# Two attention layers, one core: the masked mean taken from a copy's running sum, and layer 0's value matmuls in pairs of key groups

## The chip, the cores and the metric

The kernel runs on one core of one Trainium2 chip. The metric is device microseconds of one execution, median of several runs. TensorE (PE in the profile) does the matmuls, ScalarE (ACT) exponentials and copies, VectorE (DVE) maxima, reciprocals and sums, GpSimd (POOL) sums and powers, SyncE (SP) issues DMAs.

## The reference, cut to what matters

```
# layer 0, 8 heads of 32, x: (16, 256, 512), mask: (16, 512)
q = xt @ Wq.T                       # one projection serves as query, key and value
logits = (scores * cmask + (1 - cmask) * NEG) * rmask   # rmask: row of the query
attn = softmax(logits);  ctx = attn @ qh;  out = ctx @ Wo.T;  x = x + out
# layer 1, 16 heads of 32: rms norm, modulation, qkv, softmax(q k), o + o @ W_out;  x = x + ...
```

A row whose own mask is 0 has all logits 0, so its softmax is even over all 512 keys and its context is the plain mean of q over time. A row whose mask is 1 attends only to keys whose mask is 1. The kernel needs both: values of masked-in keys, and the mean over all of them.

## The kernel before, in words

The 16 batches go through a software pipeline of 19 iterations (-1 to 17). A steady iteration `i` (1 to 14) works on three batches at once: layer 0 attention of batch i (segments A, heads 0 to 3, and B, heads 4 to 7), layer 1 of batch i-1 (projections `qk` and `values1`, segment C), the output projection `out1` of batch i-2, and the first projection and first maxima of batch i+1. Iterations -1, 0, 15, 16 and 17 are written out on their own.

Each engine has its own queue, and its order is written out by hand, in `iteration` and its special cases. Semaphores join them. `Order` tables (BIG for the bank PX, MAXES for the four banks PM, VISITS, CONTEXT_TAKEN) turn the order into the counts to wait for; moving a call means moving its entry there.

Layer 0 of a batch: `load_x` (SP) brings x into XB and the mask into CBM. `sums_x` (L1559, VectorE) sums each row of x over time into XS. `mask_x` (L1935 GpSimd, in iteration -1 L1554 VectorE) multiplies XB by the mask. `project0` (L398, TensorE) multiplies by Wq into PX, twice (mt = 0, 1). `take_query` (ScalarE) copies PX to QF. `project_mean` (L406) multiplies the sums XS by the same weights: four matmuls of one column, eight records in the profile, since a float32 matmul shows as two. `mean0` (L1078) scales them to MEAN. `round_query` rounds QF to QHI, `split0` (L1590, VectorE) takes QLO = QF - QHI, and SP stacks both into A0 and B0 (`stack0`). `maxima0` (L422 TensorE, L1565 VectorE) bounds each row's score. `score0` (L453) makes one head's 128 keys by 512 queries, `exp0` (L1048) takes the exponential into E. `values0` (L414) transposes QF into V0.

`values_weighted0` (L480) is one visit to TensorE's tiling of 32 columns: four heads, each 128 keys by 32 columns, side by side, over one group of 128 keys; four groups in a segment add up in bank PO. `weights_summed0` (L491) and layer 1's `values_and_sums1` (L502, L505) use the same tiling. `maxima0` and `maxima1` (L431) use the tiling of 32 rows. All else uses the whole array. `add_keys0` (L1583 VectorE, L1948 GpSimd) adds the groups' E for the softmax sums. `take_sums0`, `invert0` (L1603), `scale0` (L1608, L1954) and `context0` (L1614) write the context into XB, with MEAN where the mask is 0; `out0` (L519), `residual0` (L1621), `squares` (L1157), `mean_square` (L1627), `rstd`, `norm` (L1161, L1631), `norm_rows` (L530) and `modulate` lead into layer 1.

E has three buffers for groups of keys; `buffer_free` makes `exp0` and `exp1` wait until the group held before has been visited and added.

Of the kernel before, what the change touches and what calls it, by code (L numbers as in the profile page):

```python
# [9 lines left out]
ALU = mybir.AluOpType  # L10
# [29 lines left out]
class Order:  # L40
# [29 lines left out]
    def place(self, key):  # L70
# [66 lines left out]
    (("q1", 3), 0, QUAD), (("n0", 1), 0, 0), (("tq", 0), -1, 1), (("tq", 1), -1, 2), (("s0", 0), 0, 3),  # L137
# [7 lines left out]
            (("q1", 3), 0, QUAD), (("n0", 1), 0, 0), (("tq", 0), -1, 1), (("tq", 1), -1, 2), (("s0", 0), 0, 3),  # L145
# [13 lines left out]
            (("q1", 0), 0, QUAD), (("q1", 1), 0, QUAD), (("t0", 0), 0, 0), (("q1", 2), 0, QUAD), (("t0", 1), 0, 3),  # L159
            (("q1", 3), 0, QUAD), (("n0", 1), 0, 0), (("tq", 0), -1, 1), (("tq", 1), -1, 2), (("s0", 0), 0, 3),  # L160
# [40 lines left out]
def cond_resid(nc, x, cond, cond_t, wq_t, wo_t, w_emb, b_emb_t, g_norm_t, w_qkv, g_q_t, g_k_t, w_out, out):  # L201
# [6 lines left out]
    with ctx:  # L208
# [32 lines left out]
        XS = sb("XS", [P, 2])  # L241
        MEAN = sb("MEAN", [P, 2, NB])
# [52 lines left out]
        xs_done = ev("xs_done", 1)  # L295
        xm_done = ev("xm_done", 2)
        cbi_done = ev("cbi_done", 1)
        p0_full = ev("p0_full", 3)
# [67 lines left out]
        def _(pe):  # L366
# [27 lines left out]
            def project0(i, b, mt):  # L394
                pe.wait_ge(xm_done.sem, xm_done.at(b))
                big(("p0", mt), i)
                for c in range(2):
                    last = mm(PX[:, :], WQ[:, c, mt * P:(mt + 1) * P], XB[:, c, :], start=(c == 0), stop=(c == 1))  # L398
                last.then_inc(p0_full.sem, 1)

            def project_mean(i, b):
                big(("mean", 0), i)
                pe.wait_ge(xs_done.sem, xs_done.at(b))
                for mt in range(2):
                    for c in range(2):
                        last = mm(PX[:, mt:mt + 1], WQ[:, c, mt * P:(mt + 1) * P], XS[:, c:c + 1],  # L406
                                  start=(c == 0), stop=(c == 1))
                last.then_inc(p0_full.sem, 1)
# [170 lines left out]
            def iteration(i):  # L579
# [24 lines left out]
                step_a(0, 2)  # L604
                if o1:
                    values_and_sums1(i - 1, i - 2, 3)
                if l0:
                    maxima0(i, i, 1, 0)
                step_a(0, 3)
                if l1:  # L610
                    qk(i, 1, 0)

                step_a(1, 0)
                if l1:
                    qk(i, 1, 1)
                step_a(1, 1)
                if l1:
                    qk(i, 1, 2)
                step_a(1, 2)
                if l1:  # L620
                    qk(i, 1, 3)
                step_a(1, 3)
                if l0:
                    maxima0(i, i, 1, 1)
                    values_weighted0("A", i, 0, 0)

                step_a(2, 0)
                if l1:
                    qk(i, 2, 0)
                step_a(2, 1)  # L630
                if l1:
                    qk(i, 2, 1)
                step_a(2, 2)
                if l0:
                    maxima0(i, i, 1, 2)
                if l1:
                    qk(i, 2, 2, 3)
                step_a(2, 3)
                if l0:
                    values_weighted0("A", i, 0, 1)  # L640
                    maxima0(i, i, 1, 3)

                step_a(3, 0)
                if l1:
                    qk(i, 3, 0)
                step_a(3, 1)
                if l1:
                    qk(i, 3, 1, 2)
                step_a(3, 2)
                step_a(3, 3)  # L650
                if l0:
                    rows0(i, i, 1)
                if l1:
                    qk(i, 3, 3)
                if l0:
                    values_weighted0("A", i, 0, 2)
                if p0:
                    project0(i, i + 1, 0)

                step_b(0, 0)  # L660
                step_b(0, 1)
                if l1:
                    heads_rows(i, i - 1, 0)
                    heads_rows(i, i - 1, 1)
                if p0:
                    project0(i, i + 1, 1)
                step_b(0, 2)
                if l0:
                    weights_summed0("A", i, 0)
                step_b(0, 3)  # L670

                step_b(1, 0)
                if l1:
                    heads_rows(i, i - 1, 2)
                    heads_rows(i, i - 1, 3)
                step_b(1, 1)
                step_b(1, 2)
                if l0:
                    values_weighted0("A", i, 0, 3)
                if p0:  # L680
                    project_mean(i, i + 1)
                if l1:
                    maxima1(i, i - 1, 0)
                step_b(1, 3)
                if l0:
                    values_weighted0("B", i, 1, 0)

                step_b(2, 0)
                step_b(2, 1)
                if o1:  # L690
                    out1(i, i - 2, 0, 0)
                if l1:
                    maxima1(i, i - 1, 1)
                if o1:
                    out1(i, i - 2, 0, 1, 2, 3)
                step_b(2, 2)
                if l1:
                    maxima1(i, i - 1, 2)
                if l0:
                    values_weighted0("B", i, 1, 1)  # L700
                if o1:
                    out1(i, i - 2, 1, 0, 1)
                step_b(2, 3)
                if l1:
                    maxima1(i, i - 1, 3)

                step_b(3, 0)
                if o1:
                    out1(i, i - 2, 1, 2, 3)
                step_b(3, 1)  # L710
                step_b(3, 2)
                if l1:
                    rows1(i, i - 1)
                if l0:
                    values_weighted0("B", i, 1, 2)
                if p0:
                    maxima0(i, i + 1, 0, 0)
                step_b(3, 3)
                if l1:
                    values1(i, 0, 0, 1, 2)  # L720
# [8 lines left out]
                step_c(0, 2)  # L729
                if l1:  # L730
                    values1(i, 1, 0)
                step_c(0, 3)
                if l1:
                    values1(i, 1, 1)
                if p0:
                    maxima0(i, i + 1, 0, 1)
# [3 lines left out]
                if l1:  # L740
                    values1(i, 1, 2)
                step_c(1, 2)
                if l1:
                    values1(i, 1, 3)
                step_c(1, 3)

                step_c(2, 0)
                if p0:
                    maxima0(i, i + 1, 0, 2)
                if l1:  # L750
                    values_and_sums1(i, i - 1, 0)
                if l0:
                    out0(i, i, 0)
                    out0(i, i, 1)
                step_c(2, 1)
                step_c(2, 2)
                step_c(2, 3)
                if p0:
                    maxima0(i, i + 1, 0, 3)
                if l1:  # L760
                    values_and_sums1(i, i - 1, 1)

                step_c(3, 0)
                step_c(3, 1)
                if p0:
                    rows0(i, i + 1, 0)
                step_c(3, 2)
                step_c(3, 3)
                if l0:
                    norm_rows(i, i)  # L770
                if l1:
                    values_and_sums1(i, i - 1, 2)

            def iteration_before(i):
                project0(i, i + 1, 0)
                maxima0(i, i + 1, 0, 0)
                project0(i, i + 1, 1)
# [5 lines left out]
                maxima0(i, i + 1, 0, 3)  # L783
                modulation(3)
                project_mean(i, i + 1)
                rows0(i, i + 1, 0)
                modulation(4)
                modulation(5)
                modulation(6)
                modulation(7)  # L790

            def iteration_0(i):
                values0(i, i, 0)
                score0("A", i, i, 0, 0, 0)
                score0("A", i, i, 0, 0, 1)
                maxima0(i, i, 1, 0)
                score0("A", i, i, 0, 0, 2)
                score0("A", i, i, 0, 0, 3)
                score0("A", i, i, 0, 1, 0)
                score0("A", i, i, 0, 1, 1)  # L800
                maxima0(i, i, 1, 1)
                score0("A", i, i, 0, 1, 2)
                score0("A", i, i, 0, 1, 3)
                project0(i, i + 1, 0)
                score0("A", i, i, 0, 2, 0)
                maxima0(i, i, 1, 2)
                score0("A", i, i, 0, 2, 1)
                values_weighted0("A", i, 0, 0)
                score0("A", i, i, 0, 2, 2)
                values_weighted0("A", i, 0, 1)  # L810
                maxima0(i, i, 1, 3)
# [1405 lines left out]
```

## Time and profile before

| | |
|---|---|
| median of 3 runs | 1326.3 us (1326.19 to 1329.03) |
| the profiled execution, its own time | 1324.62 us |
| its span, first to last instruction | 1322.8 us |
| mean granted TensorE clock | 0.972 of full speed |
| PE, PEld, DVE, ACT, POOL busy | 95%, 45%, 80%, 59%, 58% |
| DMA | 143.03 MB, mean 108 GB/s |

A row of the timeline names its start, its length, engine, line and operation, output and inputs, and how many instructions were merged; a matmul's end is modelled, so the distance between the starts of two rows is a better measure of what the first one takes.

### The profile page before, as it was taken

To read this page: it belongs to the slowest core of one execution; us is meant where nothing else is said; L and a number is where in the kernel's file an instruction comes from. 1 tells how busy PE (TensorE), PEld (TensorE's weight loads), DVE (VectorE), ACT (ScalarE), POOL (GpSimd) and SP (SyncE) were. 2 spreads that over 40 slices of the span, in tenths; PEclk is the share of its full clock that TensorE was granted. 3 is DMA by queue.
4 is the path that set the end of the run, shared out by engine and by line. 5 is a ranking of instruction groups with operands and counts; after the bars stand their busy time and mean duration, and the time that the engine had idled before them with its cause. 6 is when DMAs were issued, how large, how long until landed. Compare 5 with 4: busy or idle time off the path is not lost.

```text
span 1322.8 us, 20986 instructions
## 1 busy us (share of the span) xinstructions
PE 1261.4 (95%) x6896; PEld 597.6 (45%) x6896; DVE 1055.8 (80%) x934; ACT 774.6 (59%) x1377; POOL 764.4 (58%) x389
## 2 busy tenths in 40 slices
PE   6969899999999999999999999999999999999987
PEld 4424444444444454444445444444444444444433
DVE  6756778888887887888788788878888887888654
ACT  1626565665656566565656666565666656566523
POOL 0337467475746747484674748467474856638452
PEclk8859899999999999999999999999999999999999
DMA  8321534525264452626445252634525263441322
GB/s 288 105 65 47 136 105 96 140 54 151 74 148 109 99 138 56 149 72 150 107 107 131 60 147 70 153 104 112 130 60 145 69 156 100 113 110 44 97 59 70
DMA packets 77962, 143.03 MB, mean 108 GB/s; under 512 B 21536, under 2 KB 23072, under 8 KB 77856
## 3 DMA queue, kind: packets, MB, share of 16 engines
q1 hardware_dynamic: 69136, 126.17, 38.1%
q10 hardware_dynamic: 8720, 15.51, 4.0%
q8 instruction: 59, 0.97, 0.3%
q14 instruction: 47, 0.39, 0.1%
HBM read 32.02 MB, written 8.39 MB: 31 GB/s over the span
## 4 chain that ended last, share of the span: by engine, by line
PE 88%; ACT 4%; DVE 2%; issue 2%; SPq 1%; ACTq 1%; POOL 1%; DMA 0%; DVEq 0%
PE PX L541 25%; PE PS L453 11%; PE PO L480 9%; PE PX L575 8%; PE PO L502 5%; PE PS L467 4%; PE PX L398 4%; PE PM L422 4%; PE PX L519 2%; PE PM L491 2%; PE PM L519 2%; PE PM L559 2%; PE PM L431 2%; PE PO L505 2%; ACT E L1055 2%
## 5 line engine op out<-in xcount | busy, mean ns | idle before, releaser
L1048 ACT ACTIVATE E<-PS,KBIAS 128x512 f32<-128x512 f32 x512 | 345.3, 686 | 236.8 <-PE PS L453 221.9
L541 PE MATMUL PX<-WQKV,XNT 128*128 128x512 f32 x768 | 382.4, 602 | 3.4 <-ACT QK L1026 2.1
L1948 POOL TENSOR_TENSOR E<-E 128x1024 f32<-128x1024 f32 x112 | 263.4, 2359 | 160.8 <-PE PO L480 92.9
L1565 DVE TENSOR_REDUCE NM<-PM 128x4 f32<-128x2048 f32 x128 | 291.3, 2276 | 52.3 <-PE PM L422 52.3
L453 PE MATMUL PS<-B,A 97*128 97x512 f32 x512 | 301.7, 624 | 5.3 <-ACT E L1048 4.9
L1978 POOL TENSOR_TENSOR KQLO<-E 128x1024 f32<-128x1024 f32 x64 | 151.2, 2363 | 211.3 <-ACT E L1055 209.5
L1960 POOL TENSOR_TENSOR RQK<-RQK,HALF 128x16 f32<-128x16 f32 x64 | 201.0, 3148 | 28.3 <-DVE RQK L1653 27.5
L1572 DVE TENSOR_REDUCE NM<-PM 128x8 f32<-128x2048 f32 x64 | 146.6, 2291 | 49.1 <-PE PM L431 49.0
L541 PEld LDWEIGHTS PX<-WQKV,XNT 128*128 128x128 f32 x768 | 137.8, 192 | 91.4 <-issue 75.7
L1055 ACT ACTIVATE E<-PS 128x512 f32<-128x512 f32 x256 | 145.3, 596 | 49.0 <-PE PS L467 48.3
L453 PEld LDWEIGHTS PS<-B,A 97*128 97x128 f32 x512 | 95.6, 192 | 148.1 <-issue 123.6
L480 PE MATMUL PO<-E,V 128*32 128x512 f32 x1024 | 139.5, 617 | 0.0
L467 PE MATMUL PS<-B,A 97*128 97x256 f32 x512 | 124.4, 350 | 8.8 <-ACT E L1055 8.2
L1672 DVE RECIPROCAL T<-T 128x256 f32<-128x256 f32 x64 | 111.5, 1742 | 12.4 <-ACT T L1026 12.4
L575 PE MATMUL PX<-WOUT,OT 128*128 128x512 f32 x248 | 120.5, 605 | 0.0
L467 PEld LDWEIGHTS PS<-B,A 97*128 97x128 f32 x512 | 77.2, 188 | 80.2 <-issue 53.1
L1603 DVE RECIPROCAL R<-R 128x256 f32<-128x256 f32 x64 | 109.8, 1736 | 1.1
L1583 DVE TENSOR_TENSOR E<-E 128x1024 f32<-128x1024 f32 x80 | 97.7, 1238 | 11.9 <-ACT E L1048 10.1
L1935 POOL TENSOR_TENSOR XB<-XB,CBM 128x512 f32<-128x512 f32 x30 | 37.8, 1281 | 72.6 <-DVE XS L1559 56.6
L422 PE MATMUL PM<-QHI 32*128 32x512 f32 x512 | 67.1, 513 | 10.5 <-DVE NM L1565 6.9
L1646 DVE TENSOR_REDUCE SSQ<-YSQ 128x16 f32<-128x512 f32 x64 | 42.8, 669 | 40.2 <-ACT YSQ L1116 40.1
L398 PE MATMUL PX<-XB,WQ 128*128 128x512 f32 x128 | 65.6, 637 | 8.0 <-DVE XB L1554 8.0
(84 smaller groups left out, 1408.2 us busy)
## 6 DMA issues: line engine op xcount, KB each, us to landing
A<-QHI SPq DMA_DIRECT2D x256, 64.0 KB, 2.0
B<-QHI SPq DMA_DIRECT2D x256, 64.0 KB, 2.0
A<-KQHI SPq DMA_DIRECT2D x128, 128.0 KB, 2.3
B<-KQHI SPq DMA_DIRECT2D x128, 128.0 KB, 2.4
XB<-x SPq DMA_DIRECT2D x16, 512.0 KB, 3.9
A<-QLO SPq DMA_DIRECT2D x128, 64.0 KB, 2.0
B<-QLO SPq DMA_DIRECT2D x128, 64.0 KB, 2.0
X<-x ACTq DMA_DIRECT2D x16, 512.0 KB, 5.4
```

Of the source, the lines that this page charges most:

```text
L453: mm(PS[n % 2][:, :], A0[0:97, h, g * P:(g + 1) * P], B0[0:97, h, :], start=True, stop=True).then_inc(score_full, 1)
L467: last = mm(PS[n % 2][:, kb * N1:(kb + 1) * N1], A1[0:97, hq, c, kb * P:(kb + 1) * P], B1[0:97, hq, c, :], start=True, stop=True)
L480: last = mm(PO[h * DH:(h + 1) * DH, :], V0[:, q, g, h * DH:(h + 1) * DH], E[:, probs(seg, i, g), h, :], start=(g == 0), stop=(g == KB0 - 1))
L541: last = mm(PX[:, :], XNT[:, c, t * P:(t + 1) * P], WQKV[:, c, part * DM:(part + 1) * DM], start=(c == 0), stop=(c == 3))
L575: last = mm(bank, OT[:, c, t * P:(t + 1) * P], WOUT[:, c, :], start=(c == 0), stop=(c == 3))
L1048: fn(E[:, probs(seg, i, g), h, :], PS[n % 2][:, :], ACT.Exp, bias=KBIAS[:, g, b:b + 1], scale=SCALE).then_inc(exp_done, 1)
L1055: fn(E[:, probs("C", i, c), h, :], PS[n % 2][:, :], ACT.Exp, scale=SCALE_RAW).then_inc(exp_done, 1)
L1565: v.tensor_reduce(NM0[:, q, :].rearrange("p (h k) -> p h k", k=KB0)[:, :, kb], PM[:, :, :], axis=AX.X, op=ALU.max, negate=True).then_inc(m ...
L1572: v.tensor_reduce(NM1[:, :].rearrange("p (h c a) -> p h c a", c=Q1, a=2)[:, :, c, :], PM[:, :, :].rearrange("p h (a k) -> p h a k", a=2), ...
L1948: g_.tensor_tensor(running(seg, i)[:, heads_, :], running(seg, i)[:, heads_, :], E[:, probs(seg, i, g), heads_, :], ALU.add).then_inc(done, 1)
L1960: g_.tensor_tensor(rqk, rqk, HALF[:, :], ALU.pow).then_inc(rqk_done.sem, 1)
L1978: g_.tensor_tensor(key_sums(c), e[:, :, 0:N1], e[:, :, N1:2 * N1], ALU.add).then_inc(esum_done.sem, 1)
```

## The change

The mean. `project_mean`, `mean0`, `sums_x` and `mask_x` go. `project0` now multiplies x as it is; `take_query`'s copy also gives the sum of each row over time, QSUM, which is 512 times the mean of q. The mask is applied to the copy in QF, by a new `mask_query` on GpSimd, between `take_query` and `round_query`. The factor 1/512 goes into CBI.

The pairs. In iterations 1 to 14, `values_weighted0` of key groups 0 and 1 stand next to each other in TensorE's order, and so do groups 2 and 3, in both segments. Around them most of the order is written anew on all engines: on TensorE the key maxima, `qk`, `heads_rows`, `out1`, `values1`, `out0` and `values_and_sums1`; on GpSimd `scale0` ahead of segment B's sums and `rstd` behind the third `add_keys1`; on VectorE `invert0`, `invert1`, `split0` and `context1`.

```diff
-            def project_mean(i, b):
-                big(("mean", 0), i)
-                pe.wait_ge(xs_done.sem, xs_done.at(b))
...
             def project0(i, b, mt):
-                pe.wait_ge(xm_done.sem, xm_done.at(b))
+                pe.wait_ge(xin_in.sem, xin_in.at(b))
...
             def values0(i, b, mt):
-                pe.wait_ge(big_taken, BIG.upto(("p0", mt), i - 1))
+                pe.wait_ge(masked.sem, masked.at(b, mt + 1))
...
-                copy(QF[:, mt, :], PX[:, :]).then_inc(big_taken, 1)
+                fn(QF[:, mt, :], PX[:, :], ACT.Copy, accum_out=QSUM[:, mt, b:b + 1]).then_inc(big_taken, 1)
...
             def round_query(i, b, mt):
-                act.wait_ge(big_taken, BIG.upto(("p0", mt), i))
+                act.wait_ge(masked.sem, masked.at(b, mt + 1))
...
-            def mask_x(i, b):
+            def mask_query(i, b, mt):
                 pool.wait_ge(cbm_in.sem, cbm_in.at(b))
-                pool.wait_ge(xs_done.sem, xs_done.at(b))
-                for c in range(2):
-                    g_.tensor_tensor(XB[:, c, :], XB[:, c, :], CBM[:, :], ALU.mult).then_inc(xm_done.sem, 1)
+                pool.wait_ge(big_taken, BIG.upto(("p0", mt), i))
+                g_.tensor_tensor(QF[:, mt, :], QF[:, mt, :], CBM[:, :], ALU.mult).then_inc(masked.sem, 1)
```

TensorE's order in a steady iteration, the parts that the prediction speaks of:

```diff
+                step_a(2, 0)
+                if l0:
+                    values_weighted0("A", i, 0, 0)
+                    values_weighted0("A", i, 0, 1)
+                    maxima0(i, i, 1, 2)
...
+                    project0(i, i + 1, 0)
+                if l0:
+                    values_weighted0("A", i, 0, 2)
+                    values_weighted0("A", i, 0, 3)
...
+                step_b(0, 1)
+                if l0:
+                    weights_summed0("A", i, 0)
...
-                if p0:
-                    project_mean(i, i + 1)
...
+                    values_weighted0("B", i, 1, 0)
+                    values_weighted0("B", i, 1, 1)
+                if l1:
+                    maxima1(i, i - 1, 1)
...
                 if p0:
                     maxima0(i, i + 1, 0, 0)
+                if l0:
+                    values_weighted0("B", i, 1, 2)
+                    values_weighted0("B", i, 1, 3)
...
+                step_c(0, 2)
+                step_c(0, 3)
                 if l0:
                     weights_summed0("B", i, 1)
-                    values_weighted0("B", i, 1, 3)
...
+                step_c(3, 0)
+                if l0:
+                    out0(i, i, 0)
+                step_c(3, 1)
+                if l0:
+                    out0(i, i, 1)
+                if l1:
+                    values_and_sums1(i, i - 1, 1)
                 if p0:
                     maxima0(i, i + 1, 0, 3)
-                if l1:
-                    values_and_sums1(i, i - 1, 1)
-
-                step_c(3, 0)
-                step_c(3, 1)
+                step_c(3, 2)
+                if l1:
+                    values_and_sums1(i, i - 1, 2)
+                step_c(3, 3)
                 if p0:
                     rows0(i, i + 1, 0)
-                step_c(3, 2)
-                step_c(3, 3)
                 if l0:
                     norm_rows(i, i)
-                if l1:
-                    values_and_sums1(i, i - 1, 2)
```

## Rows read from the trace of the kernel before

**Rows 1.** The page's busy time: us, share of the span, instructions.

```profile
PE 1261.4 (95%) x6896; PEld 597.6 (45%) x6896; DVE 1055.8 (80%) x934; ACT 774.6 (59%) x1377; POOL 764.4 (58%) x389
```

**Rows 2.** Windows, iteration 0 and one steady: length; PE, PEld, DVE, ACT, POOL busy; clock.

```profile
36.00:99.50 63.50, 49.32 (x187) 20.09 (x187) 41.57 (x41) 27.72 (x49) 22.82 (x12) 0.69 0.31 81
...
640.42:717.39 76.97, 75.93 (x432) 35.95 (x428) 64.99 (x58) 48.29 (x86) 47.77 (x24) 1.00 0.44 111
```

**Rows 3.** Timeline of TensorE: the transposes that open iterations 2 and 14.

```profile
178.60 1.09 PE L414 MATMUL PM<-IDENT,QF 128*128 128x128 f32 x8
...
1102.32 1.09 PE L414 MATMUL PM<-IDENT,QF 128*128 128x128 f32 x8
```

**Rows 4.** Timeline of TensorE, steady iteration, around the mean's matmuls.

```profile
674.48 1.06 PE L480 MATMUL PO<-E,V 128*32 128x512 f32 x8
675.48 1.05 PE L406 MATMUL PX<-XS,WQ 128*128 128x1 f32 x8
676.46 0.50 PE L431 MATMUL PM<-KQHI 32*128 32x256 f32 x8
```

**Rows 5.** Instructions of the touched lines: ns min/median/max, first and last start.

```profile
L406 PE MATMUL PX<-XS,WQ x128: 205/250/353, 27.4 to 1138.2; 128*128 128x1 f32 x128
...
L1559 DVE TENSOR_REDUCE XS<-XB x16: 1182/1220/1221, 5.2 to 1105.3; 128x2 f32<-128x1024 f32 x16
...
L1935 POOL TENSOR_TENSOR XB<-XB,CBM x30: 1264/1282/1289, 39.3 to 1107.9; 128x512 f32<-128x512 f32 x30
...
L1157 ACT ACTIVATION_READ_ACCUMULATOR YSQ<-X x32: 184/186/202, 92.2 to 1247.9; 128x1 f32 x32
```

**Rows 6.** Timeline of ScalarE: second copy to QF and first rounding to QHI.

```profile
671.96 0.59 ACT L1026 ACTIVATE QF<-PX 128x512 f32<-128x512 f32 x1
...
688.50 0.62 ACT L1026 ACTIVATE QHI<-QF 128x512 fp32r<-128x512 f32 x1
```

**Rows 7.** Timeline of TensorE: two neighbouring column visits, then two output matmuls of iteration 17.

```profile
694.85 1.02 PE L541 MATMUL PX<-WQKV,XNT 128*128 128x512 f32 x2
695.80 1.06 PE L491 MATMUL PM<-E,ONES 128*32 128x512 f32 x8
696.69 1.04 PE L480 MATMUL PO<-E,V 128*32 128x512 f32 x8
...
1316.05 1.02 PE L575 MATMUL PX<-WOUT,OT 128*128 128x512 f32 x2
1316.91 1.02 PE L575 MATMUL PM<-WOUT,OT 128*128 128x512 f32 x2
```

**Rows 8.** The page's costliest groups: count, busy us, mean ns of one, idle before.

```profile
L1948 POOL TENSOR_TENSOR E<-E 128x1024 f32<-128x1024 f32 x112 | 263.4, 2359 | 160.8 <-PE PO L480 92.9
...
L1583 DVE TENSOR_TENSOR E<-E 128x1024 f32<-128x1024 f32 x80 | 97.7, 1238 | 11.9 <-ACT E L1048 10.1
```

**Rows 9.** Timeline: from the layer 0 output to the transposes of the norm.

```profile
705.46 1.98 PE L519 MATMUL PX<-XB,WO 128*128 128x512 f32 x4
...
710.51 0.51 PE L422 MATMUL PM<-QHI 32*128 32x512 f32 x4
710.95 1.07 PE L502 MATMUL PO<-E,V 128*32 128x256 f32 x16
...
711.07 2.29 DVE L1565 TENSOR_REDUCE NM<-PM 128x4 f32<-128x2048 f32 x1 [0.15 <-PE PM L422]
...
712.38 0.74 PE L467 MATMUL PS<-B,A 97*128 97x256 f32 x4
...
713.28 1.21 DVE L1631 TENSOR_SCALAR YSQ<-X,RSTD 128x512 f32<-128x512 f32 x1
...
714.59 1.06 PE L530 MATMUL PM<-IDENT,YSQ 128*128 128x128 f32 x8
```

**Rows 10.** Timeline, the start: ScalarE's first work and iteration 0's mean.

```profile
11.60 1.28 ACT L1026 ACT_TABLE_LOAD   x1 [11.60 <-issue]
...
66.95 1.70 PE L406 MATMUL PX<-XS,WQ 128*128 128x1 f32 x8
```

More of the change, by code:

```diff
@@ L294, in cond_resid @@
         xres_in = ev("xres_in", 16)
-        xs_done = ev("xs_done", 1)
-        xm_done = ev("xm_done", 2)
+        masked = ev("masked", 2)
         cbi_done = ev("cbi_done", 1)
-        p0_full = ev("p0_full", 3)
+        p0_full = ev("p0_full", 2)
         qhi_done = ev("qhi_done", 2)
@@ L837, in iteration_0 @@
                 score0("B", i, i, 1, 3, 0)
-                project_mean(i, i + 1)
                 score0("B", i, i, 1, 3, 1)
                 values_weighted0("B", i, 1, 1)
+                project0(i, i + 1, 1)
                 score0("B", i, i, 1, 3, 2)
@@ L868, in iteration_15 @@
+                score0("A", i, i, 0, 0, 2)
+                qk(i, 1, 0)
+                score0("A", i, i, 0, 0, 3)
+                qk(i, 1, 1)
+                score0("A", i, i, 0, 1, 0)
+                maxima0(i, i, 1, 1)
+                score0("A", i, i, 0, 1, 1)
                 qk(i, 1, 2)
+                score0("A", i, i, 0, 1, 2)
+                qk(i, 1, 3)
+                values_weighted0("A", i, 0, 0)
                 maxima0(i, i, 1, 2)
-                qk(i, 1, 3)
-                score0("A", i, i, 0, 1, 1)
@@ L899, in iteration_15 @@
                 heads_rows(i, i - 1, 0)
[L900 removed]
+                score0("B", i, i, 1, 0, 2)
+                score0("B", i, i, 1, 0, 3)
                 heads_rows(i, i - 1, 1)
[L902 to L905 removed]
+                out1(i, i - 2, 0, 2)
+                score0("B", i, i, 1, 1, 0)
                 heads_rows(i, i - 1, 2)
@@ L1251, in iteration @@
                 step_b(1, 3)
-                if p0:
-                    mean0(i, i + 1)
                 step_b(2, 0)
@@ L1320, in iteration_before @@
                 take_query(i, i + 1, 1)
+                round_query(i, i + 1, 1)
                 rows0(i, i + 1, 0)
-                mean0(i, i + 1)
-                round_query(i, i + 1, 1)
             def iteration_0(i):
@@ L1361, in iteration_0 @@
                 exp0("B", i, i, 2, 3)
+                take_query(i, i + 1, 1)
                 exp0("B", i, i, 3, 0)
-                mean0(i, i + 1)
-                round_query(i, i + 1, 1)
                 exp0("B", i, i, 3, 1)
@@ L1612, in context0 @@
                 dve.wait_ge(p0_full.sem, p0_full.at(b + 1))
-                dve.wait_ge(big_taken, BIG.upto(("mean", 0), i - 1))
-                v.scalar_tensor_tensor(out=XB[:, q, :], in0=CBI[:, :], scalar=MEAN[:, q, b:b + 1], in1=TT,
+                dve.wait_ge(big_taken, BIG.upto(("p0", q), i - 1))
+                v.scalar_tensor_tensor(out=XB[:, q, :], in0=CBI[:, :], scalar=QSUM[:, q, b:b + 1], in1=TT,
                                        op0=ALU.mult, op1=ALU.add).then_inc(ctx_done.sem, 1)
@@ L1728, in iteration @@
                 if l1:
+                    split1(i, i - 1, 1)
                     split1(i, i - 1, 2)
                     split1(i, i - 1, 3)
-                if o1:
-                    context1(i - 1, i - 2, 3)
+                if l0:
+                    invert0(i, i, 0, 1)
                 if l1:
                     maxima1(i, i - 1, 0)
-                    maxima1(i, i - 1, 1)
                 if o1:
@@ L1738, in iteration @@
                 if l1:
+                    maxima1(i, i - 1, 1)
                     maxima1(i, i - 1, 2)
-                    maxima1(i, i - 1, 3)
                 if o1:
                     residual1(i, i - 2, 1)
-                if l0:
-                    invert0(i, i, 0, 1)
+                if l1:
+                    maxima1(i, i - 1, 3)
                 if p0:
@@ L1754, in iteration @@
                     invert0(i, i, 1, 0)
-                    invert0(i, i, 1, 1)
                 if p0:
@@ L1758, in iteration @@
                 if l0:
+                    invert0(i, i, 1, 1)
                     scale0(i, i, 1)
@@ L2003, in iteration @@
                     power_heads(i, i - 1, 3)
+                if l0:
+                    masked_out(i, i)
+                if l1:
                     norm_heads(i, i - 1, 3)
+                if p0:
+                    mask_query(i, i + 1, 0)
+                    mask_query(i, i + 1, 1)
                 if l0:
+                    scale0(i, i, 0)
                     add_keys0("B", i, 1, False)
                     add_keys0("B", i, 1, True)
+                    add_keys0("B", i, 2, False)
                     add_keys0("B", i, 2, True)
-                    add_keys0("B", i, 2, False)
                     add_keys0("B", i, 3, True)
-                    scale0(i, i, 0)
                 if l1:
@@ L2014, in iteration, with iteration_before @@
                     add_keys1(i, i - 1, 1)
+                    add_keys1(i, i - 1, 2)
                 if l0:
                     rstd(i, i)
-                if l1:
-                    add_keys1(i, i - 1, 2)
+            def iteration_before(i):
+                mask_query(i, i + 1, 0)
+                mask_query(i, i + 1, 1)
             def iteration_0(i):
-                mask_x(i, i + 1)
                 add_keys0("A", i, 1, True)
@@ L2028, in iteration_0 @@
                 add_keys0("B", i, 2, False)
+                scale0(i, i, 0)
                 add_keys0("B", i, 3, True)
-                scale0(i, i, 0)
+                mask_query(i, i + 1, 1)
                 rstd(i, i)
@@ L2048, in iteration_15 @@
                 add_keys0("B", i, 2, True)
+                scale0(i, i, 0)
                 add_keys0("B", i, 2, False)
                 add_keys0("B", i, 3, True)
-                scale0(i, i, 0)
                 add_keys1(i, i - 1, 0)
@@ L2074, in _ @@
             identity()
-            pipeline(iteration, {-1: lambda i: None, 0: iteration_0, 15: iteration_15, 16: iteration_16, 17: iteration_17})
+            pipeline(iteration, {-1: iteration_before, 0: iteration_0, 15: iteration_15, 16: iteration_16, 17: iteration_17})
         @block.sync
@@ L2081, in load_x @@
                 sp.wait_ge(p0_full.sem, p0_full.at(b - 1))
-                sp.wait_ge(xm_done.sem, xm_done.at(b - 1))
+                sp.wait_ge(masked.sem, masked.at(b - 1))
                 sp.dma_start(XB[:, :, :], x_v[b]).then_inc(xin_in.sem, 16)
```

556 lines of the change are left out of this document (254 added, 302 removed), and 12 rows, old and new, of tables (BIG, special).

## The prediction

> **What bounds the kernel.** I read the page's busy times first: TensorE works 95% of the span, VectorE 80%, the other two under 60% [rows 1]. Then windows by iteration: in a steady one TensorE is busy 75.93 of 76.97 us at full clock, so 1.04 us is idle, while VectorE has 12 us free [rows 2]. Iterations 2 and 14 open at 178.60 and 1102.32 us [rows 3], twelve equal distances of 76.98. So one pattern repeats in which TensorE hardly stops: what it no longer has to do is time won, if no wait fills the gap. Iteration 0 is another case: TensorE is busy 49.32 of 63.50 us at a mean clock of 0.69 [rows 2], bound by chains through all engines.
>
> **The mean.** Its eight records take 0.98 us, from 675.48 to the next row at 676.46 [rows 4], with a column each but full weights of 128 by 128. Fourteen times gives **13.7 us**. A page of the Trainium skill speaks against this size: TensorEngine Tiling (Array Packing), "Instruction Overhead", gives a matmul of one column about 60 cycles; as an estimate from it, at 2.4 GHz, the eight would be 0.2 us and fourteen groups 2.8 us, and the sum below would come out near 1317. This trace disagrees, with 0.12 us a record.
>
> On the other engines, VectorE loses the sums, 1.22 us a batch, and masking has the same size before and after: two GpSimd operations of 1.28 us [rows 5]. I cost these at nothing, as TensorE doesn't wait for them. A copy that also sums is not in this trace; the nearest row, the read of the accumulator behind `squares`, is 0.186 us [rows 5]. Two a batch against one `mean0` leave ScalarE about level. Bounds: 0, and 32 x 0.186 = 6 us if each delayed TensorE. I take 0, since ScalarE is 59% busy [rows 1].
>
> **The mask in its new place** lies between the copy to QF and its rounding. The second copy starts at 671.96, the first rounding at 688.50 [rows 6]: 16.5 us for two masks of 1.28. Behind the masks GpSimd has `scale0` and five sums of segment B. `scale0` now comes first and waits for the second half of `invert0`, which VectorE does earlier than before, some 38 us into the iteration by my count; the first B sum could not start then anyway, since it waits for group 0's visit, at about 40. If the cover fails, B's sums are late, then `weights_summed0` of B on TensorE, then `take_sums0`, the context and `out0`. `load_x` on SP now waits for the masks instead of masked x, both long done; no DMA is added.
>
> **The pairs.** A column visit followed by another takes 0.89 us, 695.80 to 696.69 [rows 7]; followed by something else 1.00 us, 674.48 to 675.48 [rows 4]. So leaving the tiling costs 0.11 us. A full matmul takes 0.86 us, 1316.05 to 1316.91, and 0.95 when a column visit follows, 694.85 to 695.80 [rows 7]: entering a tiling from the whole array costs 0.09. Now I count calls. A steady iteration had 13 separate column blocks (A's four groups, A's sum, B's first three, B's sum with group 3, four of layer 1); afterwards it has 10 (two pairs in A, two in B, two sums, four). Stretches away from the whole array, row and column visits that touch counted as one, fall from 18 to 17. So 3 x 0.11 + 0.09 = 0.42 us an iteration, 14 x 0.42 = **5.9 us**. The column work itself stays.
>
> **What could take it back: waits in the new order.** I laid the new order out with durations of these rows. Three places are tight.
>
> (a) A's sum, about 30.5 us in. Before it VectorE has the fourth `square_sums` and the two last sums of A. `qk` 3 is done near 23.5; ScalarE copies it, does two exponentials and squares it by 26.4; 0.9 us of `square_sums` and two sums of 1.24 [rows 8] end at 29.8. Room: 0.7 us.
>
> (b) B's sum, about 55 us in. VectorE takes a maximum of 2.29 us [rows 9] from 51.3 and then the last sum of B, 1.24, until 54.8. Room: about 0.3 us there, and 3 us on GpSimd, whose five sums of 2.36 us [rows 8] run from 40 to 51.8.
>
> (c) The end. From `out0` to `norm_rows` it was 9.13 us, 705.46 to 714.59, since VectorE's `norm` stands behind a maximum, from 711.07, and then takes 1.21 us beside a GpSimd sum [rows 9]. Afterwards TensorE has some 7.9 us of work there: `out0` 4 x 0.86, layer 1's two visits 2 x 1.43 (710.95 to 712.38), maxima 0.44 (710.51 to 710.95) [rows 9], and 1.2 for three scores, row transposes and changes of tiling. The chain should shorten to about 8.7, as the third `add_keys1` now runs on GpSimd before `rstd` and not beside `norm`: 0.8 us idle, plus 0.1 ahead of `qk`, against 1.04 of before.
>
> I leave the idle time as it is. Bounds: none left (14.6 us more won), and 2.5 us an iteration (20 us back).
>
> **The start and the end.** `project0` need no longer wait for sums and mask, but ScalarE issues DMAs and loads its table until 12.9 [rows 10], so its copy comes no earlier, and the mask of 1.28 us now precedes the first rounding. Against it stand the means of iterations 0 and -1, 1.70 us at the lower clock for the first [rows 10]. The order there is new too. I take 0, bounds -3 and +4 us. Iterations 15 to 17 lose no matmul and form no pairs: 0, within 2.
>
> **Sum.** 1324.6 - 13.7 - 5.9 = 1305.0 us for the profiled execution's own time. The median is 1.7 us above it: 1306.7, of which I say **1306 us**, 20 us faster (1.5%).
>
> **Rivals.**
> 1. The end of the iteration takes back more. If `norm_rows` still comes 9.13 us after `out0` [rows 9] and A's or B's sum waits too, idle time grows by 0.5 to 1.0 us: 7 to 14 us back, 1311 to 1322. For it: three narrow places in an order written anew. Against: VectorE has 1.2 us less to do.
> 2. The idle time goes too. With half to all of the 1.04 us filled, 1291 to 1299. For: `rstd`'s new place. Against: (c).
> 3. The mean's slot is not its own: if the records are as short as their one column and the 0.98 us is two changes of tiling, 0.20 us, and a wait that stays, then 14 x (0.20 + 0.42) = 8.7 us, 1318. Against: TensorE waits for nothing between these starts [rows 4], and the records are 0.25 us long each, overlapping [rows 5]. Beside it stands the skill's 60 cycles, which would make them so short.
> 4. The change doesn't do what it says: the freed 1.4 us an iteration is spent waiting, 1324 to 1329.
> 5. Slower: (a) decides. If `qk` 3 in one block makes its copy, its squares and both last sums of A late, TensorE stands at `weights_summed0`, and B's second group of exponentials behind it, for its buffer. Every us beyond the 0.7 of room costs 14. Against the change it decides from 0.7 + 1.4 = 2.1 us late, and is over 0.2% from 2.3; at 3 us late, 1306 + 14 x 2.3 = 1338. For it: ScalarE's copy of `qk` 3 now stands ahead of A's two last exponentials. Against: VectorE's free 12 us [rows 2].
>
> **Chances.** Forecast, 1299 to 1311: 0.56. Rivals in their order: 0.17, 0.09, 0.04, 0.04, 0.10. A measurement of this kernel tells about 0.2%, 2.7 us, from no change. So faster 0.86, same 0.04, slower 0.10. The range leaves out rivals 4 and 5 and most of 2: 1298 to 1322 us.
>
> **What the profile afterwards would show.** No L406 rows, and steady iterations of about 75.6 us (76.97 - 0.98 - 0.42). Pairs of visits that take 1.89 us to the next start. TensorE's idle time near 1 us in each. VectorE busy 19.5 us less, GpSimd as before, 32 accumulator reads more. It would be wrong by a wait of L491 for sums of E (rival 5 in A, rival 1 in B), a wait of over 1 us ahead of L530, or a start longer by over 4 us, each named in the waits.

## The result, and the profile after

The kernel became slower. Over four runs each the median is 1356.43 us (1355.21 to 1357.33), against 1326.64 us for the kernel before: ratio 1.022, 95% interval 1.0202 to 1.0238. The forecast was 1306 us, with a range of 1298 to 1322 and a chance of 0.1 for slower. The profiled execution after took 1355.92 us with a span of 1354.1 us, so 31.3 us of span were added where 19.6 were to go.

The page's busy times after:

```profile
PE 1260.9 (93%) x6768; PEld 588.0 (43%) x6768; DVE 1054.3 (78%) x916; ACT 769.1 (57%) x1393; POOL 776.4 (57%) x391
```

Against [rows 1], TensorE lost its 128 records of the mean and yet is as long busy, in a span that is 31 us longer. VectorE was to be busy 19.5 us less and is only 1.5 us less. Both are the finding in short: TensorE waits, part of its work runs at a lower clock, and something on VectorE became longer by nearly as much as was taken from it.

To find the place I took the transposes that open each iteration, as [rows 3] did for before. The timeline of TensorE after, at two of them:

```profile
654.15 1.04 PE L403 MATMUL PM<-IDENT,QF 128*128 128x128 f32 x8
...
733.30 1.04 PE L403 MATMUL PM<-IDENT,QF 128*128 128x128 f32 x8
```

The same reading at all of them, with those of the experiments that follow (us of the profiled executions; the cuts are the first transposes of QF in iterations 1, 2, 14 and 15). In iteration 15 these don't open it: they stand 8.3 us behind its first `qk` before and 7.9 after, and the new order has two `qk`, two scores and one `maxima0` less in that stretch. So between the two orders only the sum of the last two columns can be compared.

| | start, to iteration 1 | iteration 1 | 2 to 13, each | 14 | 15 to the end | span |
|---|---|---|---|---|---|---|
| before | 99.66 | 78.94 | 76.98 | 85.66 | 134.82 | 1322.8 |
| after | 105.03 | 78.02 | 78.65 | 90.09 | 137.16 | 1354.1 |
| modulate first | 103.73 | 77.97 | 75.92 | 85.75 | 137.27 | 1315.7 |
| key sum waits | 102.61 | 79.60 | 75.77 | 83.24 | 139.91 | 1314.6 |
| mean alone | 101.68 | 77.92 | 76.79 | 85.48 | 132.84 | 1319.4 |
| before, swapped | 99.39 | 78.94 | 76.98 | 86.25 | 133.71 | 1322.0 |
| old start and end | 102.42 | 78.49 | 75.94 | 85.95 | 135.07 | 1313.2 |
| pairs parted | 102.65 | 79.32 | 77.40 | 87.65 | 134.24 | 1332.6 |
| mean's matmuls back | 101.31 | 79.16 | 76.52 | 89.61 | 134.40 | 1322.7 |

Steady iterations 2 to 13 account for 20.1 of the 31.3 us, the start for 5.4, and the last two columns together for 6.8; iteration 1 gives 0.9 back. The steady ones also stopped being equal. Windows of after by iteration (length; PE, PEld, DVE, ACT and POOL busy; granted clock; DMA share; GB/s):

```profile
576.07:654.15 78.08, 74.73 (x421) 34.94 (x420) 64.84 (x57) 48.11 (x87) 48.50 (x25) 1.00 0.45 109
654.15:733.30 79.15, 76.40 (x422) 35.52 (x420) 64.88 (x57) 47.72 (x87) 48.51 (x25) 0.98 0.43 107
733.30:811.13 77.83, 74.76 (x421) 34.91 (x420) 64.77 (x57) 47.77 (x87) 48.40 (x25) 1.00 0.45 109
```

The 74.7 us of work in two of these three rows is close to the forecast: 75.93 of [rows 2] less 1.4 is 74.5. What is new is idle time, 2.8 to 3.4 us in these three against 1.04, and in every second iteration (six of the twelve) 1.7 us more of busy time at a mean clock of 0.98.

TensorE's waits after (us in all, times, the longest), the first three:

```profile
PE PX L530 <- DVE XNT L1602: 27.5, 13, 2.1
PE PS L442 <- ACT E L1029: 6.2, 10, 1.4
PE PM L420 <- DVE NM L1536: 5.7, 5, 2.4
```

The line numbers have moved: L530 is now `qk`, L519 `norm_rows`, L1602 `modulate`, L1643 `context1`, L1938 GpSimd's `add_keys1`. So TensorE stands at `qk`, waiting for `modulate`, 2.1 us at the head of each of iterations 2 to 14. The timeline of after there shows why:

```profile
731.82 0.48 DVE L1595 TENSOR_SCALAR YSQ<-X,RSTD 128x512 f32<-128x512 f32 x1
...
732.21 0.69 DVE L1554 TENSOR_TENSOR QLO<-QF,QHI 128x512 fp32r<-128x512 f32 x1
...
732.65 2.47 POOL L1938 TENSOR_TENSOR KQLO<-E 128x1024 f32<-128x1024 f32 x1 [2.26 <-ACT E L1036]
...
732.81 2.58 DVE L1643 TENSOR_TENSOR OT<-T 128x256 f32<-128x256 f32 x1
...
735.32 0.98 DVE L1602 TENSOR_SCALAR XNT<-PM,AMOD,SMOD 128x256 f32<-128x256 f32 x2
...
736.45 1.96 PE L530 MATMUL PX<-WQKV,XNT 128*128 128x512 f32 x4 [2.11 <-DVE XNT L1602]
...
738.00 0.42 DVE L1643 TENSOR_TENSOR OT<-T 128x256 f32<-128x256 f32 x1
```

The same operation of VectorE, `context1`, takes 0.42 us at 738.00 and 2.58 us at 732.81. The long one began 0.16 us behind a GpSimd addition and ended at 735.39, 0.27 us behind that addition's end at 735.12. All 18 `context1` of this kernel that began while such an addition ran ended 0.28 us behind its end (0.27 here by rounded rows), and took 0.99 to 2.58 us by how much of the addition was left. So it did not run more slowly, it was held until the other was done. The new order puts it ahead of `modulate`, where before it stood behind.

Not every GpSimd operation holds it. Beside a power of `power_heads`, also from SBUF to SBUF, VectorE's operations with two SBUF inputs keep their own length: `context1` took 0.36 to 0.44 us in all 29 places of this kernel where it began during a power (in the row here two are merged), and a sum of E 1.21 to 1.24:

```profile
763.48 2.38 DVE L1547 TENSOR_TENSOR E<-E 128x1024 f32<-128x1024 f32 x2
763.65 3.81 POOL L1920 TENSOR_TENSOR RQK<-RQK,HALF 128x16 f32<-128x16 f32 x1 [0.42 <-DVE RQK L1617]
...
765.79 0.74 DVE L1643 TENSOR_TENSOR OT<-T 128x256 f32<-128x256 f32 x2
```

The kernel before already had two such rows. Its `norm` of 1.21 us in [rows 9] runs beside a GpSimd sum, and `context1` in its timeline does too:

```profile
711.83 2.38 POOL L1978 TENSOR_TENSOR KQLO<-E 128x1024 f32<-128x1024 f32 x1
713.28 1.21 DVE L1631 TENSOR_SCALAR YSQ<-X,RSTD 128x512 f32<-128x512 f32 x1
...
716.89 0.41 DVE L1679 TENSOR_TENSOR OT<-T 128x256 f32<-128x256 f32 x1
...
717.44 2.35 POOL L1978 TENSOR_TENSOR KQLO<-E 128x1024 f32<-128x1024 f32 x1 [3.24 <-ACT E L1055]
719.00 1.08 DVE L1679 TENSOR_TENSOR OT<-T 128x256 f32<-128x256 f32 x1
```

Sums that end at 714.21 and 719.79, operations of VectorE that end at 714.49 and 720.08: 0.28 and 0.29 us behind. At 716.89 `context1` was not held, as the sum began only 0.55 us behind its start.

The second loss stands right behind this stall. Here is TensorE's timeline in the iteration that opens at 654.15 and in the one that opens at 733.30, then a window of each:

```profile
657.29 3.53 PE L530 MATMUL PX<-WQKV,XNT 128*128 128x512 f32 x4 [2.11 <-DVE XNT L1602]
659.84 1.57 PE L442 MATMUL PS<-B,A 97*128 97x512 f32 x2
661.24 1.88 PE L530 MATMUL PX<-WQKV,XNT 128*128 128x512 f32 x4
...
737.84 1.03 PE L442 MATMUL PS<-B,A 97*128 97x512 f32 x2
738.71 1.88 PE L530 MATMUL PX<-WQKV,XNT 128*128 128x512 f32 x4
```

```profile
657.20:661.60 4.40, 4.30 (x7) 2.03 (x8) 2.03 (x2) 0.55 (x2) 0.00 (x0) 0.61 0.62 203
736.40:738.70 2.30, 2.25 (x6) 1.25 (x7) 1.99 (x2) 0.17 (x1) 0.00 (x0) 1.00 0.47 114
```

From the first `qk` to the second it is 3.95 us at a mean granted clock of 0.61 (0.50, the lower level of 1.2 GHz, from 658.20 to 660.20), and 2.26 us (736.45 to 738.71) at the full 2.4 GHz. The engine had done the same thing ahead of both, transposes and then 2.1 us of nothing. So one stall in two also costs 1.69 us of slow work behind it.

### The profile page after: what moved, and what is told of

Its sections match the earlier page's. It is cut to its first block, busy times and chain, and to the rows that moved or that the text cites. A ratio compares the mean times of both kernels' runs of the same rounds, so it can differ in the third digit from the quotient of the medians.

```text
span 1354.1 us, 20714 instructions
## 1 busy us (share of the span) xinstructions
PE 1260.9 (93%) x6768; PEld 588.0 (43%) x6768; DVE 1054.3 (78%) x916; ACT 769.1 (57%) x1393; POOL 776.4 (57%) x391
## 4 chain that ended last, share of the span: by engine, by line
PE 66%; DVE 11%; SPq 8%; issue 5%; ACT 3%; POOL 3%; DMA 3%; ACTq 1%; POOLq 0%; DVEq 0%
PE PX L530 24%; SPq L2060 7%; PE PS L442 7%; PE PO L469 5%; PE PS L456 5%; PE PX L564 4%; PE PM L411 4%; PE PO L491 3%; PE PX L396 3%; DVE OT L1643 3%; POOL RQK L1920 2%; PE PM L480 2%; PE PX L508 2%; PE PM L508 2%; DMA B<-KQLO 1%
## 5 line engine op out<-in xcount | busy, mean ns | idle before, releaser
L1029 ACT ACTIVATE E<-PS,KBIAS 128x512 f32<-128x512 f32 x512 | 339.6, 686 | 210.9 <-PE PS L442 199.3
L530 PE MATMUL PX<-WQKV,XNT 128*128 128x512 f32 x768 | 383.7, 617 | 30.4 <-DVE XNT L1602 27.5
L442 PE MATMUL PS<-B,A 97*128 97x512 f32 x512 | 307.7, 631 | 6.9 <-ACT E L1029 6.2
L1920 POOL TENSOR_TENSOR RQK<-RQK,HALF 128x16 f32<-128x16 f32 x64 | 211.0, 3303 | 176.5 <-DVE RQK L1617 174.9
L1938 POOL TENSOR_TENSOR KQLO<-E 128x1024 f32<-128x1024 f32 x64 | 153.1, 2392 | 204.4 <-ACT E L1036 204.4
L530 PEld LDWEIGHTS PX<-WQKV,XNT 128*128 128x128 f32 x768 | 142.6, 196 | 131.6 <-issue 118.9
L564 PE MATMUL PX<-WOUT,OT 128*128 128x512 f32 x248 | 126.9, 605 | 0.9 <-ACT QK L1007 0.9
L469 PE MATMUL PO<-E,V 128*32 128x512 f32 x1024 | 127.4, 610 | 0.0
L456 PE MATMUL PS<-B,A 97*128 97x256 f32 x512 | 117.3, 336 | 7.4 <-DMA B<-KQLO 3.3
L456 PEld LDWEIGHTS PS<-B,A 97*128 97x128 f32 x512 | 74.7, 189 | 85.8 <-issue 54.7
L396 PE MATMUL PX<-XB,WQ 128*128 128x512 f32 x128 | 68.6, 662 | 13.0 <-DMA XB<-x 5.4
L1007 ACT ACTIVATE QK<-PX 128x512 f32<-128x512 f32 x64 | 38.1, 596 | 69.3 <-PE PX L530 69.3
```

Source lines behind the costliest of these rows:

```text
L442: mm(PS[n % 2][:, :], A0[0:97, h, g * P:(g + 1) * P], B0[0:97, h, :], start=True, stop=True).then_inc(score_full, 1)
L456: last = mm(PS[n % 2][:, kb * N1:(kb + 1) * N1], A1[0:97, hq, c, kb * P:(kb + 1) * P], B1[0:97, hq, c, :], start=True, stop=True)
L469: last = mm(PO[h * DH:(h + 1) * DH, :], V0[:, q, g, h * DH:(h + 1) * DH], E[:, probs(seg, i, g), h, :], start=(g == 0), stop=(g == KB0 - 1))
L530: last = mm(PX[:, :], XNT[:, c, t * P:(t + 1) * P], WQKV[:, c, part * DM:(part + 1) * DM], start=(c == 0), stop=(c == 3))
L564: last = mm(bank, OT[:, c, t * P:(t + 1) * P], WOUT[:, c, :], start=(c == 0), stop=(c == 3))
L1029: fn(E[:, probs(seg, i, g), h, :], PS[n % 2][:, :], ACT.Exp, bias=KBIAS[:, g, b:b + 1], scale=SCALE).then_inc(exp_done, 1)
```

## The experiments

Each kernel is compared with the kernel before on the same chip. Its median there was 1325.71 us beside the first four experiments and 1325.28 us beside the last three.

**1. `modulate` first.** In the order of VectorE in a steady iteration:

```diff
                     split0(i, i + 1, 1)
-                if l1:
-                    context1(i, i - 1, 0)
                 if l0:
                     modulate(i, i)
                 if l1:
+                    context1(i, i - 1, 0)
                     invert1(i, i - 1, 1)
```

> Theory: in the changed kernel's steady iterations VectorE's first context1, which now stands ahead of modulate, runs beside a GpSimd sum and takes 2.58 us where 0.42 is usual; modulate and qk wait 2.1 us for it, and in every second iteration TensorE then runs two matmuls at the lower of its two clocks, 1.7 us more. With modulate first again (the one edit, fourteen steady iterations) the iterations should be 75.5 to 76 us, and the whole 1311 to 1318 us. Rival: the wait for modulate only hides another chain (maxima, scores, stacking DMAs), and the time stays above 1335.

Measured: 1314.86 us (1312.41 to 1317.55), ratio 0.9922, 0.9894 to 0.9949. By the medians this one exchange is worth 41.6 us (38.4 by the spans of the two profiles), and it turns 2.2% slower into 0.8% faster. The timeline there:

```profile
712.78 2.46 POOL L1937 TENSOR_TENSOR KQLO<-E 128x1024 f32<-128x1024 f32 x1 [2.41 <-ACT E L1036]
...
713.64 0.99 DVE L1602 TENSOR_SCALAR XNT<-PM,AMOD,SMOD 128x256 f32<-128x256 f32 x2 [0.60 <-PE PM L519]
714.55 0.98 DVE L1643 TENSOR_TENSOR OT<-T 128x256 f32<-128x256 f32 x1
```

`modulate` reads PM and is not held beside the same GpSimd sum (0.99 us); `context1`, which comes into the sum's last 0.69 us, ends again 0.29 us behind it, and nobody waits for that. No iteration of 2 to 13 has the lower clock's 1.7 us any more.

**2. The key sum waits.** The order of VectorE stays as changed, and only the overlap is taken away. GpSimd's fourth `add_keys1` starts behind `context1` and `modulate`. The same wait stands ahead of the one in iteration 15, which meets `context1` of iteration 14:

```diff
+                    pool.wait_ge(bank_taken[2], MAXES.upto(("t1", 1), i - 1, 2))
                     add_keys1(i - 1, i - 2, 3)
...
+                pool.wait_ge(bank_taken[2], MAXES.upto(("t1", 1), i - 1, 2))
                 add_keys1(i - 1, i - 2, 3)
```

> The changed kernel with VectorE's order kept, context1 ahead of modulate, but GpSimd's fourth key sum of layer 1 made to wait until modulate is done. If it is the overlap of the two engines that stretches context1, it takes 0.4 us again and the time is within 6 us of the kernel with modulate first, 1311 to 1322. If the position in VectorE's queue is what costs, or context1 is slow for a reason of its own, the time stays at 1350 to 1360.

Measured: 1315.73 us (1312.25 to 1318.31), ratio 0.9926, 0.9899 to 0.9953, the same as experiment 1 although `context1` stands ahead of `modulate`. Timeline:

```profile
712.25 0.42 DVE L1643 TENSOR_TENSOR OT<-T 128x256 f32<-128x256 f32 x1
...
712.94 0.99 DVE L1602 TENSOR_SCALAR XNT<-PM,AMOD,SMOD 128x256 f32<-128x256 f32 x2 [0.27 <-PE PM L519]
...
714.02 2.36 POOL L1938 TENSOR_TENSOR KQLO<-E 128x1024 f32<-128x1024 f32 x1 [4.34 <-DVE XNT L1602]
```

With GpSimd idle `context1` is back at 0.42 us. So it is the overlap that costs, and not the place in the queue as such. The sum starts 1.9 us later, seen from `norm_rows`, and delays nobody.

**3. The mean alone.** The kernel before with the first half of the change only: no sums, no `project_mean`, the mask on QF behind the last `norm_heads`; every order otherwise as before.

```diff
-                if p0:
-                    project_mean(i, i + 1)
...
+                if p0:
+                    mask_query(i, i + 1, 0)
+                    mask_query(i, i + 1, 1)
```

> The kernel before with the mean by ScalarE's copy and the masked heads alone, in the old order (masks on GpSimd behind the fourth norm_heads). By the prediction's first term it is 13.7 us faster, 1312 to 1314 us. Rival (the page's short matmuls, or a wait that fills the place): 1318 to 1326. If masking on GpSimd in the new place costs by itself, over 1327.

Measured: 1324.14 us (1321.22 to 1331.95), ratio 0.9991, 0.997 to 1.0011: no change. A steady iteration lost 0.2 us where the slot was 0.98. TensorE's waits in iterations 2 to 13, first line, and its timeline where the mean was:

```profile
PE PM L420 <- issue: 8.3, 12, 0.7
```

```profile
674.58 1.06 PE L469 MATMUL PO<-E,V 128*32 128x512 f32 x8
674.82 1.31 DVE L1629 SCALAR_TENSOR_TENSOR KQLO<-PM,GQK,KQHI 128x512 fp32r<-128x512 f32 x2
...
676.34 0.51 PE L420 MATMUL PM<-KQHI 32*128 32x256 f32 x8 [0.69 <-issue]
```

`maxima1` writes into the banks PM that VectorE's `split1` still reads until 676.13; it starts 0.21 us behind that. In [rows 4] the mean's matmuls filled this stretch. Taking them out left 0.69 us of it as a wait.

**4. Before, swapped.** Only the exchange of experiment 1, the other way, in the kernel before: `context1` of head group 0 ahead of `modulate`.

> The kernel before with context1 ahead of modulate on VectorE, as the changed kernel has it, and nothing else. There the fourth key sum starts 2.85 us behind norm_rows, after both operations, so by the overlap theory context1 stays at 0.4 us and the time at 1326 within 3 us. If the position by itself costs, about 14 x 2 us more, 1345 to 1360.

Measured: 1325.56 us (1323.77 to 1332.19), ratio 1.0012, 0.9994 to 1.0031. Iterations stay at 76.98 us. There the GpSimd sum comes only behind it (both from its timeline):

```profile
716.11 0.43 DVE L1679 TENSOR_TENSOR OT<-T 128x256 f32<-128x256 f32 x1
716.45 0.99 DVE L1638 TENSOR_SCALAR XNT<-PM,AMOD,SMOD 128x256 f32<-128x256 f32 x2
717.30 2.35 POOL L1979 TENSOR_TENSOR KQLO<-E 128x1024 f32<-128x1024 f32 x1 [3.24 <-ACT E L1055]
```

So the exchange is harmless until something else in the order brings the sum forward, relative to it, by over a microsecond. The changed order did that: there the sum starts 0.25 us behind the first of eight transposes of `norm_rows` (732.40), before 2.85 us behind it (714.59 to 717.44).

**5. Old start and end.** Experiment 1 with iterations -1, 0 and 15 to 17 in the order of experiment 3; calls are only moved, as in iteration -1 on TensorE:

```diff
-                project0(i, i + 1, 1)
...
+                project0(i, i + 1, 1)
...
+                maxima0(i, i + 1, 0, 3)
...
+                rows0(i, i + 1, 0)
...
-                maxima0(i, i + 1, 0, 3)
...
-                rows0(i, i + 1, 0)
```

> Modulate first, as in the first experiment, and besides it iterations -1, 0, 15, 16 and 17 in the order of the kernel with the mean alone (the old order). By the traces, iteration 0 took 66.6 us in the new order against 64.3 in the old, and what follows the opening of iteration 15 took 137.3 against 132.8. If these parts can be joined freely, the span is 6 to 7 us shorter than with modulate first alone: 1307 to 1310 us. Rival: their length depends on the steady iterations beside them, and the time stays within 2 us of the first experiment's 1315.

Measured: 1314.21 us (1311.64 to 1317.55), ratio 0.9914, 0.9893 to 0.9936. By its median it is the fastest kernel here, 11.1 us under the kernel before on the same chip, but it cannot be told from experiment 1, as its rival had it. The table shows a span 2.5 us shorter: start -1.3, iteration 1 +0.5, end -2.2. The expected 6 to 7 us were read off the start and the end of experiments 1 and 3, whose ends have the lower clock to different degrees (from 1270 to 1290 us a granted clock of 0.83 in experiment 1, 0.91 in experiment 3); such differences of 2 us between single profiles (132.84, 133.71, 134.82 and 135.07 for nearly the same end) decide nothing.

**6. Pairs parted.** Experiment 5 with one score between the two visits of each of the four pairs, as for the first:

```diff
                     values_weighted0("A", i, 0, 0)
+                step_a(2, 1)
+                if l0:
                     values_weighted0("A", i, 0, 1)
                     maxima0(i, i, 1, 2)
-                step_a(2, 1)
```

> The previous kernel of this call with one score between the two visits of each of the four pairs, in fourteen steady iterations, and nothing else moved. By the prediction's prices each parted pair costs one more leaving of the tiling, 0.11 us, and one more entry, 0.09: 14 x 4 x 0.20 = 11 us more than the previous kernel. Rival: the pairs are worth nothing, within 2 us of it; or they delay exponentials and parting them wins.

Measured: 1334.53 us (1333.38 to 1335.2), ratio 1.0066, 1.0045 to 1.0086, 20 us over experiment 5, where 11 were expected. By the table an iteration of 2 to 13 takes 77.40 us against 75.94, 1.46 more. The waits in iterations 2 to 13, first line:

```profile
PE PS L456 <- issue: 9.0, 12, 1.0
```

That is 0.75 us an iteration at one score of segment C, which experiment 5 doesn't have; experiment 5 has 0.2 us for GpSimd's QK in its place, which is gone here. So the parting itself costs 1.46 - 0.75 + 0.2 = 0.91 us, 0.23 a pair, against 0.20 for leaving and entering the tiling once by [rows 4, 7]. TensorE's busy time in these windows grew by 1.08 us, 0.27 a pair (75.82 against 74.74). The price of a change of tiling is of the right size, if somewhat low; the wait beside it is what a count of tilings doesn't see.

**7. The mean's matmuls back.** Experiment 5 with four matmuls of one column ahead of the second `project0`, results not used (another matmul overwrites them); no sums are taken for them, and the mean still comes from the copy.

```diff
+                if mt == 1 and 1 <= i <= 14:
+                    for m in range(2):
+                        for c in range(2):
+                            mm(PX[:, m:m + 1], WQ[:, c, m * P:(m + 1) * P], XB[:, c, 0:1], start=(c == 0), stop=(c == 1))
```

> The first kernel of this call with four matmuls of one column, of the mean's shape (their result is overwritten, so the output is unchanged), ahead of the second project0 in each of fourteen steady iterations. By the prediction's price of 0.98 us they cost 13.7 us here, since in this order TensorE waits little. If their slot is filled again by a wait, as it seems in the old order, they cost under 4 us.

Measured: 1323.74 us (1316.07 to 1327.86), ratio 0.9975, 0.9956 to 0.9994: 9.5 us over experiment 5, between the two expectations. Its timeline:

```profile
667.44 0.95 PE L398 MATMUL PX<-XB,WQ 128*128 128x1 f32 x8
668.25 1.96 PE L400 MATMUL PX<-XB,WQ 128*128 128x512 f32 x4
```

Between two whole-array matmuls the eight records take 0.81 us, 0.10 each. An undisturbed iteration grows only from 75.67 to 76.13, 0.46 us: 0.2 us of the difference is experiment 5's wait for GpSimd's QK at the transposes of `heads_rows`, which is gone here; for the other 0.15 I have no row. By the table the 9.5 us are 7.0 in iterations 2 to 13, 3.7 in iteration 14 and 0.7 in iteration 1, less 1.8 in the start and the end (rounded). Four of the twelve are 0.4 to 1.5 us longer than the others, some by a wait of `score1` for its DMA (2.9 us in four times). Iteration 14 had a granted clock of 0.96, against 1.00 in experiment 5; why stays open, so its 3.7 us can't be put down to the matmuls themselves.

## Why the prediction was wrong, point by point

**The step that failed** is the one on waits, place (c), "0.8 us idle, plus 0.1 ahead of `qk`", and with it "I leave the idle time as it is". The idle time ahead of `qk` became 2.11 us. The 0.1 us leaves room for `context1` at no more than its own 0.41 us. Neither this operation, which the new order puts ahead of `modulate`, nor GpSimd's fourth `add_keys1`, which the new order moves onto it, is named in (c). In the first half of (c) the distance was right and its parts were not: `norm_rows` came 8.65 us behind `out0` in the iteration checked (801.58 to 810.23), 8.7 forecast, but TensorE had 8.5 us of work there where 7.9 were counted, and stood still only 0.16 us where 0.8 were. I looked at `norm`'s 1.21 us beside a sum, and counted its relief as a gain, but did not ask which operation would stand beside the sum next.

The Trainium skill has the rule: SBUF — State Buffer, "Who interferes with whom", says that a VectorE instruction with two inputs in SBUF contends with a GpSimd instruction that reads SBUF, that the ports they share are an exclusive lock, and that the order of issue decides which of the two blocks. Beside GpSimd's sums the traces agree: `context1` is such an instruction, and it ended 0.28 to 0.29 us behind the sum's end in all 18 places of after and all 16 of before where a sum had begun first. The page says that `tensor_scalar` in a two-port mode fully blocks too, and `norm`, from SBUF to SBUF, ended 0.28 to 0.29 us behind the sum in 14 places of before; `modulate`, which reads PM, was not held. Beside GpSimd's powers the traces don't agree: these read SBUF as well, and `context1` kept its 0.41 us. The stall, which comes from a sum, could have been laid out by that rule and the new order.

**The clock** was in no term. The stall's direct cost in iterations 2 to 13 is 12 x (2.11 - 0.31) = 21.6 us, the slow work behind every second one 6 x 1.69 = 10.1 us; together 31.7 of the 32.8 us between after and experiment 1. Iteration 14 cost 4.3 us more; at its end TensorE waits for `modulate` 3.2 us, 1.4 in experiment 1.

**The ledger of a steady iteration** holds once the stall is away. Forecast 75.6 us; experiments 1 and 5 have 75.63 to 75.98 in most, with three or four each of 76.2 to 76.5, where `score1` waits up to 0.8 us for a DMA in some.
- The mean: 0.98 us forecast for the slot. The work in it was real, 0.81 us of records plus the change of tiling, so rival 3's short records are refuted. The Trainium skill's 60 cycles for a matmul of one column (TensorEngine Tiling (Array Packing), "Instruction Overhead"), as an estimate 0.025 us at 2.4 GHz, don't hold for these records: here it is 0.10 us each. But the other half of rival 3 was true in the old order: behind the slot stood a wait, and only 0.2 us came out (experiment 3). "TensorE waits for nothing between these starts" looked at the wrong thing: not whether the matmul waits, but whether its neighbour could start earlier.
- The pairs: 0.42 us forecast, 0.28 by the busy times. One steady window each of experiments 3 and 1, to be read against the 75.93 of [rows 2]:

```profile
333.08:409.85 76.77, 74.99 (x423) 34.99 (x419) 63.75 (x57) 48.43 (x87) 47.91 (x24) 1.00 0.44 109
```

```profile
333.45:409.14 75.69, 74.71 (x422) 34.93 (x421) 63.35 (x56) 47.97 (x87) 48.57 (x25) 1.00 0.46 112
```

  The mean takes 0.94 us of work away, but idle time grows from 1.04 to 1.78. The new order takes 0.28 us of work away, and the idle time falls back to 0.98. Two neighbouring visits took 1.85 us to the next start (748.28 to 750.13 in after), 1.89 forecast. The two halves of the change need each other: the mean gains next to nothing without the new order (experiment 3), and the new order with the mean's matmuls in it is only 1.5 us under the kernel before (experiment 7).
- Places (a) and (b), A's and B's sums, showed no stall of note in the steady iterations. So rival 5's outcome came, but not by its mechanism. Rival 1 looked at the end of the iteration, but at `norm_rows`, and not at the `modulate` and `qk` behind it.

**The start and the end** were taken as 0. In experiment 1 the start costs 4.1 us (5.4 after), and iteration 14 and the end together 2.5 (6.8 after, with the stall). At the start the bound of +4 was just reached, and passed after. Its reasoning holds in part: in experiment 3, with the old order, `project0` waits 5.6 us for x instead of 8.0 for the mask, and then `maxima0` 7.1 us for the rounding instead of 2.5. That is 2.2 us more on balance, where the start became 2.0 longer in all; other waits moved too. What the new order of the start adds is not settled: experiment 5, with the old one, gets back 1.3 us of experiment 1's 4.1. The 2.5 us are of the size by which single profiles of nearly the same end differ.

Together, in the span of experiment 1: start +4.1, iterations 2 to 13 -12.7, and the rest +1.5 (iteration 1 -1.0, iteration 14 and the end +2.5), which is -7.1 us where -19.6 was forecast. So even without the stall the forecast was too low, in this profile by 12.5 us: 4.1 from the start, 4.1 from the steady iterations (16.8 counted), and 4.3 from the rest (2.8 counted as won). By the medians, 1314.86 against 1306, it is 9 us.

## What to carry to other kernels

When an order is rewritten, lay out VectorE and GpSimd side by side, and give each VectorE operation with two SBUF inputs the end of the GpSimd sum that it meets, not its own duration (beside the powers here it kept its own); a row that is longer than its kin beside a GpSimd operation is a warning for all its kin. Before a matmul's slot is counted as won, look for what releases the instruction behind it. And a stall of 2 us of TensorE can cost half as much again (here 10.1 us on 21.6), since the clock may fall behind it.

## What was not expected of the hardware

A 128x256 product of 0.42 us, both inputs in SBUF, took 2.58 us beside a GpSimd sum of 2.47 us that had begun 0.16 us before it, and 0.41 us beside a GpSimd power of 3.81 us. A stall of 2.11 us was followed by some 3.95 us for work of 2.26 us in every second iteration, with identical work ahead of it; what picks the iterations stays open. And a float32 matmul of one column costs 0.10 us a record between full-width ones, with 128 by 128 weights loaded for each.
